# Two graph-attention layers, 64 graphs on one core: scores of the last attention in four banks, placed weight preparation, a new order of the work

## The chip, the cores and the metric

One core of a Trainium2 chip runs the whole program. The metric is device time in microseconds. TensorE (PE) multiplies matrices into PSUM, which has eight banks of 512 fp32 columns on 128 partitions; VectorE (DVE) and ScalarE (ACT) read PSUM and SBUF; GpSimd (POOL) works in SBUF alone; SyncE (SP) issues most DMAs. Each engine follows its own instruction list and waits on semaphores.

## What is computed

64 graphs of 128 nodes with 256 features each, and a 128 x 128 adjacency matrix for each graph. For each graph:

```python
h = relu(layernorm(x))
# first layer (GAT): 4 heads of 128; scores = leaky_relu(asrc + adst), masked, softmax; elu
# second layer (GAT): 1 head of 256, the same with other weights
x = x + gat2(elu(gat1(h)))
h = relu(layernorm(x))
# multi-head attention: 8 heads of 32, masked by adj
q, k, v = h @ Wq, h @ Wk, h @ Wv
out = relu(softmax(mask(q k^T / sqrt(32))) @ v)
x = x + out @ Wo
```

## The kernel before

The work on one graph is cut into some 75 small functions, each on one engine: `project1` (h times W1), `transpose_ab`, `scores1_mask`, `scores1`, `transpose1`, `aggregate1`, `project2`, `scores2`, `transpose2`, `aggregate2`, `qk`, `project_v`, `scores3_mask`, `scores3_first`, `scores3_last`, `mha_av`, `project_out` on TensorE. Between them ACT and DVE take results out of PSUM and do softmax, and GpSimd does a power for the layer norm (`rsqrt1`, `rsqrt2`), masks, a normalisation (`normalise`), a diagonal matrix (`diagonal2`) and the rounding of the exponentials (`e3_first_halves`, `e3_last_halves`).

Each engine runs one loop of steps. A hand-written list gives the order of its functions in a step and, as a number, the phase: in step t a function with phase p works on graph t - p. So each step works on up to a dozen graphs, and the order in a list is the order in which that engine issues. The steps of two engines are not tied to each other but by semaphores: `done` waits for the same graph's input, `free` for a buffer of a ring of two, and `after(pe, sem, g, lag)` for what has to have been read out of a PSUM bank before the function writes to it.

Matrix products in fp16 use numbers split into a high and a low half (`SPLIT`, three products for each). The halves of h, h2, the attention output and the exponentials e3 are turned by DMA transposes on SP's queue (`norm1_transpose`, `norm2_transpose`, `att_transpose`, `e3_transpose_first` and `_last`).

The last attention runs as follows. `qk` makes q and k transposed in one bank; `qk_copy` (ACT, L487) writes their high half and `qk_low` (DVE, L724) the low half; `scores3_mask` writes the mask into two banks, `scores3_first` and `scores3_last` add the scores of four heads each. A head has 32 channels, so its matmul uses a strip of 32 of the array's rows, and the two banks take turns:

```python
for col in columns:
    for n, (i, j) in enumerate(SPLIT):
        for b in range(2):
            h = head_at(4 * b + col)
            r = slice(DK * (h % 4), DK * (h % 4 + 1))
            pe.matmul(S[:, b, col * N:(col + 1) * N], qkT[r, ...], qkT[r, ...])
```

`mha_max` (DVE, L756 and L761) takes the maxima of all eight heads, `mha_exp_first` and `mha_exp_last` (ACT, L497) the exponentials, the e3 halves (POOL, L372 and L374) split them, and `mha_av` multiplies with v. `relu2` (ACT, L482) takes z from `norm2_apply` (DVE, L631), which follows `residual1` (L738), `norm2_moments` and `variance2`.

The weights are prepared in the first steps, by functions that stand between two steps (`before={...}`): `prepare_w1` and `prepare_w2` find the largest weight (`power_of_two`, with two small matmuls of `spread_largest`), scale and split.

## Time and profile before

| | |
|---|---|
| median of 3 runs | 776.16 us (776.13 to 776.79) |
| profiled execution | 774.69 us, its span 772.6 us |
| TensorE busy | 716.3 us, 93% of the span, 8398 matmuls |
| weight loads busy | 593.4 us, 77% |
| DVE busy | 681.4 us, 88% |
| ACT busy | 591.6 us, 77% |
| GpSimd busy | 515.8 us, 67% |
| mean DMA rate | 110 GB/s |

The span is the stretch that the profiler records, from the first instruction to the last. Matmuls overlap, so the duration of one is longer than its share of the time; the spacing of starts is what counts. ACT and DVE instructions overlap a little too: the next starts some 0.1 us before the one before ends.

### The profile page before, as it was taken

The numbers are of one execution on the slowest core, as the hardware profiler recorded it, in microseconds if no ns is written. First come the engines' busy times: TensorE is split into PE (matmuls) and PEld (weight loads), VectorE is DVE, ScalarE is ACT, GpSimd is POOL, SyncE is SP. The second block draws the span as 40 slices with busy tenths as digits, with TensorE's granted clock in tenths as the row PEclk, the third lists the DMA queues.
The fourth block names the chain that finished last, engine by engine and source line by source line (L and its number), as shares of the span: only waits on it lengthen the run. The fifth ranks groups of instructions, "written<-read, shape, count | busy, mean of one in ns | idle before, by whom it ended". The sixth has DMA issues, their size and how long they took to land.

```text
span 772.6 us, 26496 instructions
## 1 busy us (share of the span) xinstructions
PE 716.3 (93%) x8398; PEld 593.4 (77%) x8398; DVE 681.4 (88%) x2017; ACT 591.6 (77%) x1865; POOL 515.8 (67%) x733
## 2 busy tenths in 40 slices
PE   0389999999999999999999999999999999999973
PEld 0157788888888888888888888888888888788852
DVE  4758899999999999999999999999999989999873
ACT  0167888888888778888888788788888888788752
POOL 5456777676767676667667766676677767766551
PEclk9999999999999999999999999999999999999996
DMA  6111555666578566557766656766655666655464
GB/s 197 33 37 43 106 112 112 121 110 118 118 117 115 116 112 113 119 114 115 122 110 118 112 124 115 115 110 120 114 119 116 113 119 106 112 118 105 89 110 89
DMA packets 270423, 84.70 MB, mean 110 GB/s; under 512 B 242896, under 2 KB 269904, under 8 KB 270288
## 3 DMA queue, kind: packets, MB, share of 16 engines
q1 hardware_dynamic: 270288, 83.02, 57.8%
q8 instruction: 70, 1.15, 0.7%
q14 instruction: 65, 0.53, 0.3%
HBM read 15.86 MB, written 8.39 MB: 31 GB/s over the span
## 4 chain that ended last, share of the span: by engine, by line
PE 75%; DVE 9%; DMA 5%; issue 4%; SPq 3%; ACT 1%; POOL 1%; DVEq 0%; ACTq 0%; POOLq 0%
PE bank L815 28%; PE bank L840 11%; PE bank L986 7%; PE bank L947 6%; DMA hT<-h_split 4%; PE bank L966 3%; PE bank L929 3%; PE bank L936 3%; PE bank L866 3%; PE bank L891 2%; PE bank L889 2%; PE bank L881 2%; SPq L276 1%; DVE top L756 1%; PE bank L874 1%
## 5 line engine op out<-in xcount | busy, mean ns | idle before, releaser
L497 ACT ACTIVATE e<-bank,nmx,q_power 128x128 f32<-128x128 f32 x512 | 194.7, 481 | 5.1 <-DVE nmx L761 5.1
L372 POOL CAST e_split<-e 128x512 f16<-128x512 f32 x128 | 82.4, 643 | 118.6 <-ACT e L497 118.6
L374 POOL TENSOR_TENSOR e_split<-e,e_split 128x512 f16<-128x512 f32 x128 | 151.7, 1185 | 10.3
L840 PE MATMUL bank<-w,h1T 128*128 128x258 f32 x512 | 122.8, 382 | 0.7 <-DVE shift L599 0.7
L386 POOL TENSOR_TENSOR rstd<-var,minus_half 128x1 f32<-128x1 f32 x128 | 71.7, 560 | 66.6 <-DVE var L625 66.6
L815 PE MATMUL bank<-w_split,hT 128*128 128x260 f16 x768 | 98.2, 278 | 12.3 <-DMA hT<-h_split 11.9
L840 PEld LDWEIGHTS bank<-w,h1T 128*128 128x128 f32 x512 | 96.6, 190 | 16.6 <-DVE h1T L655 1.6
L448 ACT ACTIVATE eT<-lr,nmx 128x128 f32<-128x128 f32 x256 | 102.7, 458 | 0.8 <-DVE nmx L713 0.8
L815 PE MATMUL bank<-h2T,proj_split 128*128 128x128 f16 x1536 | 97.4, 220 | 1.6 <-DMA h2T<-h_split 1.6
L815 PEld LDWEIGHTS bank<-h2T,proj_split 128*128 128x128 f16 x1536 | 92.0, 99 | 3.7 <-DMA h2T<-h_split 2.4
L815 PEld LDWEIGHTS bank<-w_split,hT 128*128 128x128 f16 x768 | 71.1, 98 | 24.5 <-issue 7.0
L364 POOL TENSOR_TENSOR eTn<-eT,rs 128x512 f32<-128x512 f32 x64 | 67.0, 1046 | 17.9 <-DVE rs L752 17.9
L756 DVE TENSOR_REDUCE top<-bank 128x8 f32<-128x1024 f32 x64 | 77.3, 1208 | 0.3 <-PE bank L947 0.3
L424 ACT ACTIVATE h_split<-z 128x256 f16<-128x256 f32 x64 | 26.6, 416 | 65.9 <-DVE z L631 65.9
L947 PEld LDWEIGHTS bank<-qkT 32*128 32x128 f16 x1536 | 43.0, 93 | 37.7 <-issue 36.0
L986 PE MATMUL bank<-en,xl 128*128 128x128 f32 x512 | 68.3, 276 | 0.2
L448 ACT ACTIVATION_READ_ACCUMULATOR eT<-lr,nmx 128x1 f32 x256 | 65.7, 257 | 0.0
L947 PE MATMUL bank<-qkT 32*128 32x128 f16 x1536 | 64.8, 216 | 0.3 <-DVE qkT L724 0.2
L986 PEld LDWEIGHTS bank<-en,xl 128*128 128x128 f32 x512 | 62.2, 192 | 2.0 <-ACT en L455 1.3
L604 DVE SCALAR_TENSOR_TENSOR h_split<-z,h_split 128x256 f16<-128x256 f32 x128 | 61.5, 481 | 0.6 <-ACT h_split L424 0.5
L815 PE MATMUL bank<-proj_split,attT 128*128 128x256 f16 x384 | 54.3, 279 | 6.1 <-DMA attT<-att_split 6.1
L440 ACT ACTIVATE lr<-bank,ab 128x128 f32<-128x128 f32 x64 | 23.5, 368 | 43.6 <-PE bank L867 43.6
(116 smaller groups left out, 1921.7 us busy)
## 6 DMA issues: line engine op xcount, KB each, us to landing
x_in<-in_x_dram SPq DMA_DIRECT2D x64, 128.0 KB, 2.3
out_dram<-x_out SPq DMA_DIRECT2D x64, 128.0 KB, 2.0
adj_in<-in_adj_dram SPq DMA_DIRECT2D x64, 64.0 KB, 2.5
e3T<-e_split SPq DMA_TRANSPOSE x128, 3.1
hT<-h_split SPq DMA_TRANSPOSE x64, 2.4
h2T<-h_split SPq DMA_TRANSPOSE x64, 2.5
attT<-att_split SPq DMA_TRANSPOSE x64, 2.8
w<-in_L_gnn_W_dram SPq DMA_DIRECT2D x2, 256.0 KB, 3.1
```

What stands on the lines that cost most here:

```text
L364: pool.tensor_tensor(eTn[:, g.two, :].rearrange("p (h n) -> p h n", h=H), eT[:, g.two, :].rearrange("p (h n) -> p h n", h=H), rs[:, g.two, ...
L372: pool.tensor_copy(e3_split[:, g.two, half, 0], e).then_inc(s[high_set], 1)
L374: pool.tensor_tensor(e3_split[:, g.two, half, 1], e, e3_split[:, g.two, half, 0], ALU.subtract).then_inc(s[low_set], 1)
L386: pool.tensor_tensor(rstd[:, g.two, which:which + 1], var[:, g.two, which:which + 1], minus_half[:, :], ALU.pow).then_inc(s[rstd_set], 1)
L448: ins = act.activation(eT[:, g.two, h * N:(h + 1) * N], lr[:, g.two, h * N:(h + 1) * N], ACT.Exp, bias=nmx[:, g.two, h:h + 1], accum_out=s ...
L497: ins = act.activation(e3[:, g.two, h, :], S[:, h // 4, (h % 4) * N:(h % 4 + 1) * N], ACT.Exp, bias=nmx3[:, g.two, h:h + 1], scale=q_power ...
L604: dve.scalar_tensor_tensor(out=out_, in0=in_, scalar=0.0, in1=high_, op0=ALU.max, op1=ALU.subtract).then_inc(s[sem_], 1)
L756: dve.tensor_reduce(top3[:, g.two, :], S.rearrange("p b (h n) -> p (b h) n", h=4), AX.X, ALU.max, negate=True).then_inc(s["top3_set"], 1)
L815: ins = pe.matmul(out_, left, right, start=n == 0, stop=n == len(pairs) - 1)
L840: ins = pe.matmul(X2[:, 0:D + 2], h1T[:, g.two, k * F:(k + 1) * F], w2[:, k, :], start=k == 0, stop=k == H - 1)
L947: ins = pe.matmul(S[:, b, col * N:(col + 1) * N], qkT[r, g.two, i, h // 4, :], qkT[r, g.two, j, 2 + h // 4, :], start=False, stop=n == 2 a ...
L986: ins = pe.matmul(O1[:, h * N:(h + 1) * N], xl[:, g.two, h * F:(h + 1) * F], en[:, g.two, h * N:(h + 1) * N], start=True, stop=True)
```

## The change

**Scores in four banks.** S becomes the first half of banks 0 to 3. Bank b takes the two heads whose channels lie in row strip b, so four consecutive matmuls use four strips and four banks. Half a score stage is one half of the heads (0 to 3, 4 to 7). The other tiles are given other banks: some that had a bank for themselves now share one.

**Order.** All five lists are new, and phases with them. TensorE's first function is now `project1`, with phase 0. `scores3_first` and `scores3_last` stand side by side, between `transpose1` and `aggregate1`.

**Weight preparation** is cut into functions with a place of their own in the lists, each run once, at graph 0. W1 is loaded first; the attention vectors and b1 of the first layer go by ACT's queue and have their own semaphores.

```diff
-        XL = bank[:, 0:2, :]
-        ABT = bank[:, 2, 0:N // 2].bitcast(F16)
-        Z = bank[:, 3]
+        XL = bank[:, 4:6, :]
+        ABT = bank[:, 1, 0:N // 2].bitcast(F16)
+        Z = bank[:, 7]
         ET = bank[:, 6]
-        O1 = bank[:, 1]
+        O1 = bank[:, 6]
         X2 = bank[:, 6]
-        Z2 = bank[:, 7]
-        ET2 = bank[:, 6]
-        O2 = bank[:, 2]
-        QK = bank[:, 7]
-        V = bank[:, 3]
-        S = bank[:, 4:6, :]
-        AV = bank[:, 2]
-        WO = bank[:, 0]
...
+        Z2 = bank[:, 3]
+        ET2 = bank[:, 4]
+        O2 = bank[:, 4]
+        QK = bank[:, 6]
+        V = bank[:, 4]
+        S = bank[:, 0:4, 0:2 * N]
+        AV = bank[:, 7]
+        WO = bank[:, 5]
...
             steps(lambda graphs: run([
-                (e3_transpose_last, 9), (att_transpose, 10), (store, 11), (norm1_transpose, 3), (e3_transpose_first, 8),
-                (load_adj, 1), (load_x, 0), (norm2_transpose, 6),
+                (norm2_transpose, 8), (e3_transpose_last, 9), (load_adj, 4), (norm1_transpose, 4), (e3_transpose_first, 9),
+                (att_transpose, 10), (load_x, 0), (store, 11),
             ], graphs))
...
-                (e3_last_halves, 9), (masks, 3), (e3_first_halves, 8), (rsqrt1, 2), (rsqrt2, 6), (diagonal2, 5),
-                (normalise, 4),
...
+                (masks, 6), (split_low2, 10), (rsqrt1, 4), (rsqrt2, 9), (split_low3, 11), (split_low0, 9),
+                (e3_last_halves, 10), (split_low1, 9), (products_w2, 5), (picks, 2), (products_w1, 2), (diagonal2, 8),
+                (e3_first_halves, 10), (normalise, 7),
...
-                (v_copy, 9), (relu1, 3), (gat2_leaky, 6), (att_copy, 10), (abT_copy, 4), (gat1_copy, 5), (gat2_exp, 6),
-                (gat1_leaky, 4), (mha_exp_first, 8), (elu_exp, 5), (gat2_copy, 6), (mha_exp_last, 8), (qk_copy, 7),
-                (gat1_exp, 4), (relu2, 6),
...
+                (gat1_copy, 7), (gat1_leaky, 6), (elu_exp, 7), (relu2, 8), (split_high0, 7), (mha_exp_last, 9),
+                (split_high2, 8), (mha_exp_first, 9), (gat1_exp, 6), (abT_copy, 5), (gat2_leaky, 7), (relu1, 3), (v_copy, 9),
+                (gat2_exp, 7), (qk_copy, 8), (gat2_copy, 7), (split_high1, 7), (att_copy, 10), (split_high3, 8),
...
-                (xl2_evac, 6), (relu2_low, 7), (ab_high, 4), (v_low, 9), (ab_low, 4), (xl_evac, 4), (gat2_scores, 6),
-                (mha_max, 8), (att_low, 10), (relu1_low, 3), (residual2, 11), (norm1_moments, 2), (gat1_scores, 4), (elu, 5),
-                (gat2_recip, 6), (variance1, 2), (residual1, 6), (norm2_moments, 6), (variance2, 6), (qk_low, 7),
-                (ab2_evac, 5), (norm2_apply, 6), (gat1_recip, 4), (att_norm, 9), (norm1_apply, 2),
...
+                (v_low, 10), (proj_largest, 7), (relu1_low, 4), (gat2_recip, 8), (qk_low, 9), (w1_sums, 2), (att_low, 11),
+                (residual1, 8), (proj_row, 7), (w1_largest, 0), (w1_row, 3), (w2_shift, 7), (w1_scale, 4), (norm2_moments, 8),
+                (variance2, 8), (mha_max, 9), (norm2_apply, 8), (proj_scale, 7), (elu, 7), (relu2_low, 8), (b1_prep, 5),
+                (gat1_scores, 6), (ab_high, 5), (ab_low, 5), (w2_sums, 5), (xl_evac, 5), (norm1_apply, 3), (w1_products, 0),
+                (ab2_evac, 7), (att_norm, 10), (residual2, 11), (xl2_evac, 7), (variance1, 2), (norm1_moments, 1),
+                (gat1_recip, 6), (gat2_scores, 7),
...
             def scores3_mask(g):
                 done(pe, s["masks_set"], g)
-                after(pe, s["e3_last"], g, -1)
-                wide = mask_mha[:, g.eight, :].unsqueeze(1).to_broadcast((128, 4, N))
-                for b in range(2):
-                    ins = pe.matmul(S[:, b, :].rearrange("p (h n) -> p h n", h=4), ident16[:, :], wide, start=True, stop=False)
+                after(pe, s["e3_first"], g, -1)
...
+                wide = mask_mha[:, g.eight, :].unsqueeze(1).to_broadcast((128, 2, N))
+                for b in range(4):
+                    ins = pe.matmul(S[:, b, :].rearrange("p (h n) -> p h n", h=2), ident16[:, :], wide, start=True, stop=False)
                 ins.then_inc(s["s_mask"], 1)
...
+                for n, (i, j) in enumerate(SPLIT):
+                    for b in range(4):
+                        r = slice(DK * b, DK * (b + 1))
+                        ins = pe.matmul(S[:, b, chunk * N:(chunk + 1) * N], qkT[r, g.two, i, chunk, :], qkT[r, g.two, j, 2 + chunk, :],
+                                        start=False, stop=n == 2 and chunk == 1)
...
             steps(lambda graphs: run([
-                (scores3_mask, 8), (scores3_first, 8), (scores2, 6), (scores3_last, 8), (transpose_ab, 4), (transpose1, 5),
-                (scores1_mask, 4), (scores1, 4), (project_out, 11), (aggregate1, 5), (transpose2, 6), (project_v, 8), (qk, 7),
-                (aggregate2, 6), (project2, 5), (mha_av, 9), (project1, 3),
-            ], graphs), before={0: lambda: spread_largest(0, 0, 2, 2), 4: lambda: spread_largest(1, 2, 6, 3)})
+                (turn_w1, 0), (spread_w1, 0), (project1, 0), (project2, 2), (w2_ones, 1), (project_out, 6), (transpose_ab, 0),
+                (project_v, 4), (scores2, 2), (qk, 3), (scores3_mask, 3), (transpose2, 2), (scores1_mask, 0), (scores1, 0),
+                (aggregate2, 2), (transpose1, 1), (turn_proj, 1), (scores3_first, 3), (scores3_last, 3), (aggregate1, 1),
+                (mha_av, 4), (spread_proj, 1),
+            ], graphs))
```

## Rows read from the trace of the kernel before

**Rows 1.** The chain that ended last, at two places: start us, us, what.

```profile
77.11 1.00 PE bank L815 x9
...
714.70 1.34 PE bank L815 x12
```

**Rows 2.** Timeline of PE: start us, us, engine, line, operation, out<-in, shape, count.

```profile
26.00 2.76 PE L815 MATMUL bank<-w_split,hT 128*128 128x260 f16 x12 [6.99 <-DMA hT<-h_split]
...
207.95 1.49 PE L815 MATMUL bank<-w_split,hT 128*128 128x260 f16 x12
209.27 0.59 PE L936 MATMUL bank<-mask_mha,ident 128*128 128x512 bf16 x2
209.80 0.51 PE L947 MATMUL bank<-qkT 32*128 32x128 f16 x12
210.24 0.49 PE L866 MATMUL bank<-diag,ones 128*128 128x128 f32 x2
...
211.22 0.60 PE L966 MATMUL bank<-ident,eTn 128*128 128x128 f32 x4
...
218.81 1.49 PE L815 MATMUL bank<-w_split,hT 128*128 128x260 f16 x12
```

**Rows 3.** Timeline of ACT in the same step.

```profile
208.26 0.42 ACT L482 ACTIVATE h_split<-z 128x256 f16<-128x256 f32 x1
208.58 0.37 ACT L492 ACTIVATE vv<-bank 128x256 f16<-128x256 f32 x1
...
211.86 0.60 ACT L455 ACTIVATE en<-bank 128x512 f32<-128x512 f32 x1 [0.16 <-PE bank L966]
212.36 0.39 ACT L471 ACTIVATE eT<-lr,nmx 128x128 f32<-128x128 f32 x1
...
212.74 0.68 ACT L433 ACTIVATE lr<-bank,power 128x512 f32<-128x512 f32 x1
...
215.41 1.55 ACT L497 ACTIVATE e<-bank,nmx,q_power 128x128 f32<-128x128 f32 x4
216.78 0.67 ACT L487 ACTIVATE qkT<-bank 128x512 f16<-128x512 f32 x1
217.26 0.48 ACT L448 ACTIVATE eT<-lr,nmx 128x128 f32<-128x128 f32 x1
...
218.71 0.26 ACT L448 ACTIVATION_READ_ACCUMULATOR eT<-lr,nmx 128x1 f32 x1
```

**Rows 4.** Timeline of DVE in the same step.

```profile
211.69 1.21 DVE L756 TENSOR_REDUCE top<-bank 128x8 f32<-128x1024 f32 x1
212.93 0.32 DVE L761 TENSOR_SCALAR nmx<-top,q_power 128x8 f32<-128x8 f32 x1
213.16 0.41 DVE L766 TENSOR_TENSOR att_split<-att,att_split 128x256 f16<-128x256 f32 x1
...
216.66 0.48 DVE L738 SCALAR_TENSOR_TENSOR x<-bank,rs,x_in 128x256 f32<-128x256 f32 x1 [0.42 <-PE bank L929]
217.18 0.43 DVE L617 BATCH_NORM_STATS2 stats<-x 128x6 f32<-128x256 f32 x1
...
217.94 0.69 DVE L724 TENSOR_TENSOR qkT<-bank,qkT 128x512 f16<-128x512 f32 x1
```

**Rows 5.** The tile z: durations in ns, min/median/max, first and last start us.

```profile
L631 DVE TENSOR_SCALAR z<-x,mv,rstd x64: 404/646/673, 58.1 to 743.6; 128x256 f32<-128x256 f32 x64
```

**Rows 6.** The page's costliest groups: busy us, mean ns of one, idle before.

```profile
L372 POOL CAST e_split<-e 128x512 f16<-128x512 f32 x128 | 82.4, 643 | 118.6 <-ACT e L497 118.6
L374 POOL TENSOR_TENSOR e_split<-e,e_split 128x512 f16<-128x512 f32 x128 | 151.7, 1185 | 10.3
```

**Rows 7.** The page's DMA issues: count, median us from issue to landing.

```profile
e3T<-e_split SPq DMA_TRANSPOSE x128, 3.1
```

**Rows 8.** Timeline of SP's queue.

```profile
215.50 1.19 SPq L263 DMA_TRANSPOSE hT<-h_split  x1
```

**Rows 9.** The chain that ended last, in the first 30 us.

```profile
4.19 6.85 DMA b_all<-in_L_gnn_b_dram
```

More of the change, by code:

```diff
@@ L231, in run, with once, first @@
                     function(graphs[phase])
+        def once(function):
+            def first(g):
+                if g.n == 0:
+                    function(g)
+            return first
         block = ctx.enter_context(nc.Block())
@@ L333, in picks, with products_w1 @@
                                        pattern=[[-H, 2], [-1, 2], [0, 128]], channel_multiplier=1).then_inc(s["pick_set"], 1)
-            def products_w1():
-                pool.wait_ge(s["w1_in"], 16 * 5)
+            @once
+            def products_w1(g):
+                pool.wait_ge(s["w1_in"], 16 * KD)
+                pool.wait_ge(s["att1_in"], 16 * 2)
                 for k in range(KD):
@@ L549, in prepare_w1, with rows_of_largest @@
-            def prepare_w1():
-                dve.wait_ge(s["w1_in"], 16 * 5)
-                dve.wait_ge(s["ident_set"], 5)
-                dve.tensor_reduce(largest[:, 0:1], w1[:, :, :, high], AX.XYZ, ALU.max, apply_absolute_value=True).then_inc(s["largest_set"], 1)
+            def rows_of_largest(n, first, last):
+                rows, column = last - first, list(turned).index(n)
+                dve.wait_ge(turned[n], 1)
+                dve.tensor_reduce(row_largest[0:rows, column:column + 1], PREP[n][0:rows, 0:128], AX.X, ALU.max).then_inc(row_set[n], 1)
+                dve.wait_ge(row_set[n], 1)
+                dve.tensor_scalar(largest_diag[0:rows, first:last], ident[0:rows, 0:rows], row_largest[0:rows, column:column + 1], None,
+                                  ALU.mult).then_inc(diag_set[n], 1)
@@ new lines, in powers_of_two @@
+            def powers_of_two(n, first, last):
+                dve.wait_ge(spread[n], 1)
+                dve.tensor_scalar(power[:, first:last], PREP[n][:, 128:128 + last - first], 2.0 ** -60, None, ALU.max).then_inc(power_set[n], 1)
+                dve.wait_ge(power_set[n], 1)
+                bits = power[:, first:last].bitcast(I32)
+                dve.tensor_scalar(bits, bits, 0x7f800000, None, ALU.bitwise_and).then_inc(power_set[n], 1)
+                dve.wait_ge(power_set[n], 2)
+                dve.tensor_scalar(scale[:, first:last].bitcast(I32), bits, -1.0, float(254 << 23), ALU.mult, ALU.add).then_inc(scale_set[n], 1)
@@ L553, in prepare_w1, with w1_largest, w1_products @@
+            @once
+            def w1_largest(g):
+                dve.wait_ge(s["w1_in"], 16 * KD)
+                dve.tensor_reduce(largest[:, 0:1], w1[:, :, :, high], AX.XYZ, ALU.max, apply_absolute_value=True).then_inc(s["largest_w1"], 1)
+            @once
+            def w1_products(g):
+                dve.wait_ge(s["w1_in"], 16 * KD)
+                dve.wait_ge(s["att1_in"], 16 * 2)
                 for k in range(KD):
@@ L785, in _, with turn_w1 @@
         @block.tensor
         def _(pe):
[L787 removed]
+            @once
+            def turn_w1(g):
                 pe.wait_ge(s["ident_set"], 5)
[L790 to L796 removed]
@@ new lines, in turn_proj, with spread_proj @@
+            @once
+            def turn_proj(g):
+                pe.wait_ge(s["ident_set"], 5)
+                pe.wait_ge(s["largest_proj"], 1)
+                at_ends(pe, s["e3_first"], g, -2)
+                pe.transpose(PREP["proj"][0:4, 0:128], largest[:, 2:6], ident[:, :]).then_inc(turned["proj"], 1)
+            @once
+            def spread_proj(g):
+                pe.wait_ge(s["ones_set"], 4)
+                pe.wait_ge(diag_set["proj"], 1)
+                pe.matmul(PREP["proj"][:, 128:132], ones[0:4, :], largest_diag[0:4, 2:6], start=True, stop=True).then_inc(spread["proj"], 1)
```

253 lines of the change are left out of this document (157 added, 96 removed).

## Prediction

> **What bounds the kernel now.** I read the page first (TensorE is busy for 93% of the span), then the chain that ended last, then one graph's step on each engine in order of time. The long middle is a pipeline with one graph per step: the first projection of graph 5 starts at 77.1 us and that of graph 63, the last, at 714.7 [rows 1], so 58 steps take 637.6 us, 10.99 each. A step in which TensorE's rows show no idle time takes 218.81 - 207.95 = 10.86 us [rows 2]. The 0.13 on top comes in single late steps. So the step is set by TensorE's issue order. Around it lie 77.1 us of fill and 772.6 - 714.7 = 57.9 us of drain. The reader should see three parts: 77.1 + 58 x 10.99 + 57.9 = 772.6, the span. The profiled execution took 774.69, so 2.1 lie outside the span, and the median of the runs (776.16) is 1.5 above that.
>
> **How full is a step?** TensorE has slack nowhere, but another loop is nearly as long. Scores need q and k rounded by ACT and DVE, the maximum needs the scores, the exponentials need the maximum, and ACT rounds the next graph's q and k only after them. Before: the maximum starts at 211.69, that graph's exponentials are followed by qk_copy at 216.78 (5.09 later, 0.67 long), qk_low starts at 217.94, and the next maximum 10.86 - (217.94 - 211.69) = 4.61 after that [rows 3, 4]. 5.09 + 0.67 + 4.61 = 10.37: this loop has only some 0.5 us of slack. That number decides the case.
>
> **Four strips.** Twelve strip matmuls take 210.24 - 209.80 = 0.44 us, with a change of tiling in it. Columns go by at one price: twelve matmuls of 260 columns take 209.27 - 207.95 = 1.32, 0.11 each, so 128 columns are 0.055 and two of 512 are 0.43. The entry gap is then 209.80 - 209.27 - 0.43 = 0.10 [rows 2]. Six pairs at 0.055 are 0.33, and the exit 0.10. So pairs overlap fully today. With four strips and four banks it would be three rounds for a half, six instead of twelve for a graph: 6 x 0.055 = 0.33 us saved. The trace shows no four at once; the lower bound is no gain, the upper 0.33. I take 0.33, since pairs reach the full factor of two. scores2 no longer stands between the halves, so two of the four tiling changes go: 2 x 0.10 = 0.20. The mask goes from two matmuls of 512 columns to four of 256: the same columns, nothing. TensorE's own step: 10.86 - 0.33 - 0.20 = 10.33.
>
> **The wait that takes part of it back.** aggregate1 reads en, which ACT copies after transpose1. Today scores1_mask, scores1 and project_out lie between them. In the new order only the two score halves do. transpose1 starts at 211.22, the copy ends at 211.86 + 0.60 = 212.46 [rows 2, 3], 1.24 after. New: four transposes 0.44 (512 columns of fp32 at twice the price) + change 0.10 + scores 0.33 + change 0.10 = 0.97, so 0.27 of waiting. With no gain from four strips it would be 1.30 and no waiting. So whether four strips overlap moves the step by only 0.06: TensorE's step is between 10.60 and 10.66.
>
> **The other loop in the new order.** I lay out all that stands in it, from the start of the maximum. DVE: maximum 1.24 (212.93 - 211.69), nmx3 0.23 (213.16 - 212.93) [rows 4]; then norm2_apply, which now stands between them and ACT's exponentials, because relu2 is placed ahead of mha_exp_last and needs z: 0.40 to 0.65 (shortest and median) [rows 5]; handover 0.04. ACT: relu2 0.32 (208.58 - 208.26), eight exponentials 2 x 1.37 = 2.74 (216.78 - 215.41), gat1_exp 218.71 - 217.26 + 0.09 = 1.54, abT_copy 0.15 (estimate, a short copy; at most gat2_leaky's), gat2_leaky 0.27 (an estimate: as v_copy), relu1 0.32 (as relu2), v_copy 0.27 (its 0.37 less the overlap of 0.10 that relu2's rows show), gat2_exp 0.38 (212.74 - 212.36), qk_copy 0.67 [rows 3]: together 6.66. gat1_exp and relu2 stood behind qk_copy before; now they stand ahead. DVE again: handover 0.03, qk_low 0.60 (its 0.69 less the 0.09 by which nmx3's successor overlaps it), att_low 0.34 (an estimate: a 256-column operation of 0.41, as its row has it, less 0.07), residual1 0.52 (217.18 - 216.66), moments and variance 217.94 - 217.18 = 0.76 [rows 4]: 2.25 with the handover. The shortest loop is 1.24 + 0.23 + 0.41 + 0.04 + 6.66 + 2.25 = 10.83, with the median z it is 11.07. So qk_low no longer has 4.61 us of DVE work behind it, but 2.2; from the maximum's start to the end of qk_copy it is 1.92 + 6.66 = 8.58, where it was 5.09 + 0.67 = 5.76. This loop, not TensorE, sets the new step. I take 10.95, the middle. TensorE then idles some 0.3 to 0.6 us a step, mostly at scores3_first (qkT) and aggregate1 (en).
>
> By the Trainium skill (SBUF — State Buffer, section "Who interferes with whom") a DVE tensor_scalar in a two-port mode and a GpSimd instruction lock each other out of a shared port pair. The spread of z between 0.40 and 0.65 agrees with that. In the new order GpSimd has rsqrt2 behind it and waits for mha_exp_last when norm2_apply runs, so by that rule z would take 0.41 and the step would be 10.83, 7 us less over 58 steps than my sum.
>
> **Other moved work that I cost at nothing.** hT is now transposed more than a step ahead of project1, which takes away the late steps (the 0.13). The e3 halves take 0.64 + 1.19 each on GpSimd [rows 6] and their transposition lands 3.1 after issue [rows 7]; the last lands near the start of mha_av, see the rivals. ABT, Z2, XL, V, O2 and ET2 now share banks with other tiles, but their evacuations lie a step earlier, in DVE and ACT time that is in the loop already.
>
> **Fill.** Today DVE waits for w1_in until 4.19 + 6.85 = 11.04, the landing of b1's broadcast, which w1_in counts though nothing of W1 needs it [rows 9]; the first projection starts at 26.0 [rows 2], 15 later. New: W1 goes first, the attention vectors and b1 go by ACT's queue, b1 has its own semaphore, the first maximum needs W1 alone, and relu1_low is placed ahead of the splits, so hT's DMA is hidden by them. I take 4 from the earlier start and 3 from the hidden relu1_low and DMA: project1 at 19. The five steps after it take 77.1 - 26.0 = 51.1; there DVE stands in line for GpSimd's prod2 products. Placed in pieces, each needed later, I take 4 off, between 0 and 8. In all 11, so graph 5 at 66. The bounds are 3 (the broadcasts still late, the placed pieces as long) and 15. **Drain.** project1 is now first in its step, not last, but there are three steps fewer behind it: 57.9 as before, plus or minus 3.
>
> **Sum.** 66 + 58 x 10.95 + 57.9 = 759.0; with 2.1 and 1.5 it is 762.6, and I say 762.
>
> **Rivals.** (1) TensorE stays the bound and all of its saving comes through, at 10.65: the loop through ACT is shorter than I sum, since no row shows these neighbours together. 66 + 617.7 + 57.9 + 3.6 = 745. For it: TensorE alone is bound today. Against: the loop today was found from the same rows and fits. (2) The shared port rule holds at each step: 10.83, so 755.6. (3) Slower: mha_av waits. exp_last is done at 1.92 + 0.32 + 1.37 + 0.13 = 3.7 after the maximum's start, GpSimd does the last half until 5.6, diagonal2, then the first until 7.9; SP issues norm1_transpose (1.19) ahead of it [rows 8], so issue at up to 9.0 and landing at 12.1. mha_av's place is near 11.4. What is late there goes through project1, project2, project_out, project_v and qk to qk_copy, that is into the loop; over two steps it adds half of what it is late. At a step of 11.3 the time is 66 + 655.4 + 57.9 + 3.6 = 783. It decides from (776.2 - 3.6 - 123.9)/58 = 11.18 on, so when the landing is later by another 0.5. (4) The middle as I say and the fill shortened by 4 only: 770. (5) The change does not do what it says: four strips go by two at a time. By the terms above the time is the same, because aggregate1 waits for en anyway; only a trace tells it from my forecast.
>
> **How the numbers follow.** Forecast (10.9 to 11.05 a step) 0.40, (1) 0.20, (2) 0.15, (3) 0.15, (4) 0.10; (5) has 0.3, inside the others. The range 743 to 778 takes in (1), (2), (4) and the near half of (3). Below 0.2% (1.6 us) this kernel's runs cannot tell a change. Faster 0.83, same 0.04, slower 0.13.
>
> **What the profile would show.** Right: strip matmuls in 0.35 a graph with nothing between the halves; TensorE idle in the middle with qkT (DVE) and en (ACT) as releasers; step 10.9 to 11.0; first project1 near 19, graph 5 near 66. Wrong: a step under 10.7, or waits of mha_av for the e3T DMA at the head of the list, or graph 5 after 72.

## The result, and the profile after

The changed kernel takes 831.9 us (830.08 to 834.44, 4 runs) beside 776.14 (775.66 to 776.79) for the kernel before on the same chip: 1.072 times as long, 95% interval 1.069 to 1.075. The forecast was 762, range 743 to 778. The sign was wrong. All times are medians of executions in the faster of the chip's two states; one execution of b1_et_bank5 (969 us, granted clock 0.705) fell in the slower state and is left out.

The page of the changed kernel: span, busy time, then the chain by engine and by line.

```profile
span 830.5 us, 27002 instructions
...
PE 718.0 (86%) x8526; PEld 583.0 (70%) x8526; DVE 706.6 (85%) x2017; ACT 598.5 (72%) x1865; POOL 510.9 (62%) x733
...
PE 30%; DMA 19%; DVE 13%; POOL 11%; ACT 10%; issue 9%; SPq 8%; POOLq 0%; ACTq 0%; DVEq 0%
```

TensorE's busy time hardly moved (716.3 before), its share fell from 93% to 86%. VectorE's grew by 25.2 us (681.4 before), and the rounding of the normalised rows alone grew by 25.9 (L693: 87.4 us, where the same instruction, L604 of the kernel before, took 61.5). The rest of the longer span is waiting. The chain names no one engine: DMA, GpSimd and SP's queue hold 38% of it together. That is how a kernel looks whose step is set by loops through several engines.

The first projections, from TensorE's timeline (graph 0, graph 5) and from the chain (graph 63), which answer to [rows 1] and the first row of [rows 2]:

```profile
24.65 2.57 PE L925 MATMUL bank<-w_split,hT 128*128 128x260 f16 x11 [7.64 <-DVE w_split L645]
...
75.23 1.38 PE L925 MATMUL bank<-w_split,hT 128*128 128x260 f16 x11
```

```profile
769.52 1.34 PE bank L925 x12
```

Between graphs 5 and 63 lie 694.3 us, 11.97 a step. The 57.9 us by which the span grew are: fill 75.2 - 77.1 = -1.9, 58 steps x (11.97 - 10.99) = +56.7, drain 61.0 - 57.9 = +3.1. So it is the step. A step is the time from one graph's first projection to the next one's; fill is what lies before graph 5, drain what lies behind graph 63.

The chain that ended last, 25 us from the middle (start us, us, what):

```profile
305.70 1.23 SPq L274
306.99 3.66 DMA adj_in<-in_adj_dram
310.72 0.54 POOL absent L433
...
312.52 1.06 POOL rstd L418 x2
313.60 0.43 DVE z L720
...
314.72 1.15 ACT e L550 x3
...
316.62 1.22 POOL e_split L406
317.85 1.23 SPq L274
```

It closes on itself: e3_transpose_last (L274) at 305.70 and again at 317.85, 12.15 later. In between: SP issues load_adj behind e3_transpose_last, the adjacency lands, GpSimd makes the masks from it, both rsqrt stand behind the masks in GpSimd's list, norm2_apply needs rsqrt2, ACT's exponentials stand behind relu2 which needs z, GpSimd splits the exponentials, and only then can SP issue the next e3_transpose_last. The masks wait for the load in 37 of the 64 graphs, so not every step is 12.15: single steps lie between 10.87 and 13.23, and the mean is 11.97. SP's next row, behind its 1.23 for e3_transpose_last:

```profile
319.13 0.57 SPq L265 DMA_DIRECT2D adj_in<-in_adj_dram  x1
```

The load itself waits for nothing of this; it only stands behind an instruction that does. Phases 4 (load_adj on SP) and 6 (masks on GpSimd) look like two steps of lead. But SP's list has e3_transpose_last with phase 9 and GpSimd's has e3_last_halves with phase 10: SP's step waits for GpSimd's next one. So it is one step, and since the load stands behind that instruction and the masks stand first in the next step, nothing is left of it. Before, both halves had the same phase on both engines (9), and load_adj 1 against masks 3 was two steps.

The longest waits that this and the next loop cause (engine line <- releaser: us in total, times, longest us):

```profile
POOL absent L433 <- DMA adj_in<-in_adj_dram: 41.0, 37, 2.1
PEld bank L967 <- DMA e3T<-e_split: 38.9, 42, 4.0
```

TensorE's timeline around the scores, to be held against the score row of [rows 2]:

```profile
406.79 0.52 PE L1074 MATMUL bank<-qkT 32*128 32x128 f16 x24
407.64 1.13 PE L1115 MATMUL bank<-en,xl 128*128 128x128 f32 x8 [0.33 <-ACT en L508]
```

24 strip matmuls take what 12 took before (0.51): with 0.21 for the last one alone, the starts are (0.52 - 0.21)/23 = 0.013 apart instead of (0.51 - 0.21)/11 = 0.027. Four strips do overlap, and aggregate1 waits 0.33 for en. The ends of matmuls are modelled in a profile, but for the last graph the maximum waits for them, 0.57 after their first start at 810.01:

```profile
810.58 1.22 DVE L843 TENSOR_REDUCE top<-bank 128x8 f32<-128x1024 f32 x1 [0.29 <-PE bank L1074]
```

### The profile page after: what moved, and what is told of

Read it like the earlier page. It is cut to its first block, busy times and chain, and to the rows that moved or that the text cites. A ratio compares the mean times of both kernels' runs of the same rounds, so it can differ in the third digit from the quotient of the medians.

```text
span 830.5 us, 27002 instructions
## 1 busy us (share of the span) xinstructions
PE 718.0 (86%) x8526; PEld 583.0 (70%) x8526; DVE 706.6 (85%) x2017; ACT 598.5 (72%) x1865; POOL 510.9 (62%) x733
## 4 chain that ended last, share of the span: by engine, by line
PE 30%; DMA 19%; DVE 13%; POOL 11%; ACT 10%; issue 9%; SPq 8%; POOLq 0%; ACTq 0%; DVEq 0%
PE bank L925 13%; DMA e3T<-e_split 11%; DMA adj_in<-in_adj_dram 7%; ACT e L550 7%; PE bank L954 5%; POOL e_split L406 4%; SPq L274 4%; DVE top L843 3%; POOL e_split L404 2%; SPq L280 2%; DVE z L720 2%; POOL rstd L418 2%; PE bank L1054 2%; ACT eT L501 1%; PE bank L1065 1%
## 5 line engine op out<-in xcount | busy, mean ns | idle before, releaser
L404 POOL CAST e_split<-e 128x512 f16<-128x512 f32 x128 | 77.9, 609 | 176.2 <-ACT e L550 176.2
L550 ACT ACTIVATE e<-bank,nmx,q_power 128x128 f32<-128x128 f32 x512 | 184.4, 464 | 2.6 <-DVE nmx L848 2.6
L954 PEld LDWEIGHTS bank<-w,h1T 128*128 128x128 f32 x512 | 92.9, 192 | 17.1 <-DVE h1T L744 5.2
L1115 PE MATMUL bank<-en,xl 128*128 128x128 f32 x512 | 72.3, 284 | 23.5 <-ACT en L508 23.5
L508 ACT ACTIVATE en<-bank 128x512 f32<-128x512 f32 x64 | 38.2, 597 | 74.2 <-PE bank L1093 74.1
L693 DVE SCALAR_TENSOR_TENSOR h_split<-z,h_split 128x256 f16<-128x256 f32 x128 | 87.4, 683 | 0.5 <-ACT h_split L535 0.5
L513 ACT ACTIVATE ex<-bank,minus_one 128x512 f32<-128x512 f32 x64 | 44.0, 687 | 49.0 <-PE bank L1115 49.0
L967 PE MATMUL bank<-vv,e3T 128*128 128x33 f16 x512 | 46.1, 179 | 30.8 <-DMA e3T<-e_split 30.3
L967 PEld LDWEIGHTS bank<-vv,e3T 128*128 128x128 f16 x512 | 40.4, 96 | 39.0 <-DMA e3T<-e_split 38.9
L433 POOL TENSOR_SCALAR absent<-adj_in 128x128 f32<-128x128 int32 x64 | 39.3, 614 | 41.5 <-DMA adj_in<-in_adj_dram 41.0
```

What stands on the lines that cost most here:

```text
L404: pool.tensor_copy(e3_split[:, g.two, half, 0], e).then_inc(s[high_set], 1)
L550: ins = act.activation(e3[:, g.two, h, :], S[:, h % 4, (h // 4) * N:(h // 4 + 1) * N], ACT.Exp, bias=nmx3[:, g.two, 2 * (h % 4) + h // 4:2 ...
L693: dve.scalar_tensor_tensor(out=out_, in0=in_, scalar=0.0, in1=high_, op0=ALU.max, op1=ALU.subtract).then_inc(s[sem_], 1)
L954: ins = pe.matmul(X2[:, 0:D + 2], h1T[:, g.two, k * F:(k + 1) * F], w2[:, k, :], start=k == 0, stop=k == H - 1)
L967: pe.matmul(AV[:, o:o + DK + 1], e_high, vv[:, g.two, 0, h, :], start=True, stop=False)
L1115: ins = pe.matmul(O1[:, h * N:(h + 1) * N], xl[:, g.two, h * F:(h + 1) * F], en[:, g.two, h * N:(h + 1) * N], start=True, stop=True)
```

## The experiments

Times are in us, with the ratio to the kernel before on the same chip and its 95% interval. Kernels with the same letter ran on one chip; the kernel before took 776.1 beside the changed kernel, 774.1 beside a, 774.0 beside b, 775.5 beside c, 774.4 beside e and 773.3 beside f. So up to 3 us of a difference between two letters can be the chip's.

| kernel | us | ratio |
|---|---|---|
| after | 831.9 | 1.072 (1.069 to 1.075) |
| a1_adj_step_earlier | 818.6 | 1.057 (1.053 to 1.060) |
| a2_adj_before_e3 | 809.3 | 1.046 (1.043 to 1.049) |
| a3_two_strips | 824.9 | 1.068 (1.063 to 1.072) |
| a4_adj_two_strips | 821.8 | 1.062 (1.057 to 1.067) |
| b1_et_bank5 | 830.4 | 1.074 (1.069 to 1.079) |
| b2_adj_et_bank5 | 808.6 | 1.045 (1.042 to 1.048) |
| b3_adj_et_two_strips | 809.0 | 1.046 (1.043 to 1.049) |
| b4_before_halves_together | 772.3 | 0.998 (0.997 to 0.999) |
| c1_relu1_low_moved | 820.2 | 1.058 (1.056 to 1.061) |
| c2_relu2_behind | 935.6 | 1.207 (1.204 to 1.211) |
| c3_c2_adj_back | 937.4 | 1.208 (1.205 to 1.212) |
| c4_products_w2_later | 807.2 | one run |
| e1_xl2_early | 800.6 | 1.035 (1.031 to 1.039) |
| e2_c1_xl2_early | 802.1 | 1.036 (1.033 to 1.040) |
| e3_xl2_adj_back | 828.4 | 1.071 (1.067 to 1.076) |
| e4_relu1_low_behind_qk | 808.7 | 1.047 (1.041 to 1.052) |
| f1_e3_ahead_of_norm1 | 801.8 | 1.039 (1.033 to 1.045) |
| f2_e3_ahead_xl2_early | 797.7 | 1.033 (1.030 to 1.036) |

### The adjacency's place

a2 puts the load ahead of the transposition it stood behind; a1 leaves it there and issues it a step earlier.

```diff
-                (norm2_transpose, 8), (e3_transpose_last, 9), (load_adj, 4), (norm1_transpose, 4), (e3_transpose_first, 9),
+                (norm2_transpose, 8), (load_adj, 4), (e3_transpose_last, 9), (norm1_transpose, 4), (e3_transpose_first, 9),
```

```diff
-                (norm2_transpose, 8), (e3_transpose_last, 9), (load_adj, 4), (norm1_transpose, 4), (e3_transpose_first, 9),
+                (norm2_transpose, 8), (e3_transpose_last, 9), (load_adj, 3), (norm1_transpose, 4), (e3_transpose_first, 9),
```

> The changed kernel with load_adj kept at phase 4, but placed ahead of e3_transpose_last in SyncE's list instead of behind it. Theory A: the load no longer waits for the rounding of the exponentials, so it is issued about 1.5 us or more earlier and the loop is cut at the same place: as with a step earlier, 775 to 795 us. If it is not the order in the queue but the landing time of the load itself that is long (3.7 us in the middle, beside a median of 2.2), the step falls by less than half of that. Theory B: 825 to 835 us.

> The changed kernel with one number changed: load_adj has phase 3 in place of 4 on SyncE, so each adjacency matrix is loaded one step earlier; the ring of four has room for it. Theory A (a loop through SyncE's queue sets the step: e3_transpose_last, load_adj behind it, landing, masks, rsqrt1 and rsqrt2, norm2_apply, relu2, mha_exp_last, e3_last_halves, e3_transpose_last): that loop is cut, the step falls from 11.97 to the next loop, 11.0 to 11.3, and the time from 832 to 775 to 795 us. Theory B (mha_av waiting for the landing of the first e3 transposition, rival 3 of the prediction, costs the step): nothing of it is touched, 825 to 835 us.

a2 gives back 22.6 us, a1 13.3 (20 and 12 by the ratios). Both miss the 775 to 795 that theory A gave them, and the 825 to 835 of theory B. In both the masks' wait for the adjacency is gone from the head of the list of waits. What a1 has first among waits for a DMA, against 38.9 in the changed kernel:

```profile
PEld bank L967 <- DMA e3T<-e_split: 37.1, 37, 3.8
```

So in a1 mha_av's wait for the transposed exponentials, my rival 3, is left nearly whole. In a2 it falls to 16.8 us (18 times), and a2 is the faster one by 9.3. a1 keeps load_adj's 0.57 in SP's queue ahead of e3_transpose_first, a2 does not; that fits, though no run separates it from the rest.

e3 and c3 put the load back into two later kernels.

> e1 with load_adj behind e3_transpose_last again, as the change has it. The adjacency loop (e3_transpose_last 1.23, adjacency landing 3.67, masks and both rsqrt on GpSimd, z, relu2, the three exps, e_split, e3_transpose_last again) has nothing of xl2_evac in it: 11.9 to 12.1 a step, 826 to 834. If xl2_evac's place was part of what made the adjacency loop long, it is faster than 820.

> The kernel before it in this list with load_adj back behind e3_transpose_last, as in the change. Its loop (e3_transpose_last, load_adj, landing, masks, rsqrt1, rsqrt2, norm2_apply, relu2) still ends in relu2, but mha_exp_last is no longer behind relu2, so the loop is cut on ACT's side: 0 to +8 us over that kernel. If GpSimd's own order carries it on (rsqrt2, then e3_last_halves): +15 to +30 us.

e3 is 27.8 us above e1 and near the changed kernel: with the load at its new place, what else was mended is not seen. c3 is as c2 within their spread (937.4 and 935.6): where another loop is longer (13.7 a step there), the place costs nothing. In these two pairs loops do not add; the longest counts.

### Strips and halves

```diff
-                for n, (i, j) in enumerate(SPLIT):
-                    for b in range(4):
+                for n, (i, j), b in [(n, ij, b) for pair in ((0, 1), (2, 3)) for n, ij in enumerate(SPLIT) for b in pair]:
+                    if True:
```

> The changed kernel with the strip matmuls of scores3 issued for banks 0 and 1 first and then for banks 2 and 3, so that two strips at most run side by side; nothing else. TensorE's score stage grows by 0.33 us a graph. Theory A: TensorE is not in the loop that sets the step, so 0 to +6 us (830 to 838). Rival: what TensorE does longer is paid in full, 64 x 0.33 = +21 us (853).

> load_adj one step earlier and two strips at a time together. Against the kernel with load_adj one step earlier alone: by the prediction's own sum 0.06 us a step at most, since aggregate1 waits for en anyway: 0 to +4 us. Rival: with the adjacency loop cut TensorE is the bound again and all 0.33 us is paid: +21 us.

> As the kernel before it in this list (ET in bank 5, load_adj ahead), and the strip matmuls two at a time. Theory C with the prediction's sum: the score stage is 0.33 us longer, TensorE is not in the loop, 0 to +4 us. Rival (TensorE is now the bound): +15 to +21 us.

None is slower than its partner by more than the spread (824.9 beside 831.9, 821.8 beside 818.6, 809.0 beside 808.6). But the three kernels did not do what their names say. a3's rows, in a step and for the last graph, where the scores start at 802.91:

```profile
414.97 0.53 PE L1074 MATMUL bank<-qkT 32*128 32x128 f16 x24
```

```profile
803.51 1.22 DVE L843 TENSOR_REDUCE top<-bank 128x8 f32<-128x1024 f32 x1 [0.33 <-PE bank L1074]
```

The 24 starts are as dense as with four strips in turn (0.52), and the maximum that waits for them starts 0.60 after the first, where the changed kernel has 0.57. Two strips at a time would have made that 0.90, by my own 0.33. The list gives six matmuls to strips 0 and 1 before six to strips 2 and 3, and yet they overlap nearly as four. How TensorE comes to that, by taking work out of the list's order or by strips that work off queues of their own, is not shown: the rows do not say which strip a start belongs to. So these runs say nothing of what two at a time would cost. That it costs little rests on the wait of 0.33 behind the scores alone.

b4 takes the kernel before and moves scores2 from between the score halves to ahead of them.

```diff
-                (scores3_mask, 8), (scores3_first, 8), (scores2, 6), (scores3_last, 8), (transpose_ab, 4), (transpose1, 5),
+                (scores2, 6), (scores3_mask, 8), (scores3_first, 8), (scores3_last, 8), (transpose_ab, 4), (transpose1, 5),
```

> The kernel before, and only TensorE's order of scores2 changed: it stands ahead of scores3_mask, so that the two halves of the scores follow each other and two of four changes of tiling go. The prediction's sum says 0.20 us a graph, and since TensorE's issue order sets the step of that kernel, 64 x 0.20 = 13 us faster (762 us beside 775); a rival: the loop with 0.5 us of slack and late hT transpositions take it back, 0 to -5 us.

It saves 1.7 us (0.2%), not 13, and lies in the range of the rival (0 to 5 us). The halves are together (timeline):

```profile
407.78 1.08 PE L947 MATMUL bank<-qkT 32*128 32x128 f16 x24
```

Without a gap, 24 starts 0.027 apart and the last one's 0.21 make 0.83; the row has 1.08. The second half waits for the first (the semaphore s_half; the weight loads idle for it 64 times, 15.1 us in all, 0.24 each), since in the two-bank layout its strips write the banks that the first half's other strips write. Before, scores2 filled that time. So most of the 0.20 that I expected of two tiling changes is lost to this wait, and joining the halves is worth 0.2% alone. In the new layout each bank has one strip, and the wait is left out; no run says what joining is worth there.

### Banks

b1 and b2 take ET out of bank 6 (b1 from the changed kernel, b2 from a2).

```diff
-        ET = bank[:, 6]
+        ET = bank[:, 5]
...
-                after(pe, s["qkT_set"], g, -2)
-                at_ends(pe, s["ab2_set"], g, -1)
-                at_ends(pe, s["xl2_set"], g, -1)
+                after(pe, s["x_out_set"], g, -5)
+                after(pe, s["xl_set"], g, 1)
```

> The changed kernel with ET (what transpose1 writes) in bank 5 in place of bank 6, so that transpose1 no longer waits until qk_low has read q and k out of the bank it shares with them, but for the read of WO a step earlier; the load of the adjacency stays where the change put it. Theory C (two loops of nearly the same length: one through SyncE's queue, 12.0 us, one through bank 6: qk_low, transpose1, gat1_copy, aggregate1, elu_exp, relu2, exponentials, gat1_exp, qk_copy, qk_low, 11.5 to 11.8 us): cutting the second alone leaves the first, 820 to 833 us. Theory D (bank 6 alone is the cost): 775 to 795 us.

> ET in bank 5 and load_adj ahead of e3_transpose_last in SyncE's list together. Theory C: both loops are cut and the step falls to the loop that the prediction laid out (maximum, norm2_apply, relu2, exponentials, gat1_exp, qk_copy, qk_low), 10.9 to 11.2 us; with 73 us of fill and 61 of drain 768 to 785 us. If the bank was no cost, it stays at the 809 us of the kernel with load_adj moved alone.

Neither moves anything (830.4 beside 831.9; 808.6 beside 809.3). ET's bank is not what holds the step.

### VectorE's order: relu1_low, relu2, xl2_evac

c1 moves relu1_low from between v_low and qk_low to behind relu2_low (from b2); c2 also moves relu2 behind mha_exp_last on ACT.

```diff
-                (v_low, 10), (proj_largest, 7), (relu1_low, 4), (gat2_recip, 8), (qk_low, 9), (w1_sums, 2), (att_low, 11),
+                (v_low, 10), (proj_largest, 7), (gat2_recip, 8), (qk_low, 9), (w1_sums, 2), (att_low, 11),
...
-                (variance2, 8), (mha_max, 9), (norm2_apply, 8), (proj_scale, 7), (elu, 7), (relu2_low, 8), (b1_prep, 5),
+                (variance2, 8), (mha_max, 9), (norm2_apply, 8), (proj_scale, 7), (elu, 7), (relu2_low, 8), (relu1_low, 4), (b1_prep, 5),
```

```diff
-                (gat1_copy, 7), (gat1_leaky, 6), (elu_exp, 7), (relu2, 8), (split_high0, 7), (mha_exp_last, 9),
+                (gat1_copy, 7), (gat1_leaky, 6), (elu_exp, 7), (split_high0, 7), (mha_exp_last, 9), (relu2, 8),
```

> The kernel with both loops cut (load_adj ahead of e3_transpose_last, ET in bank 5; 809 us, step 11.34 where undisturbed and 11.6 on average), and on DVE relu1_low moved from ahead of qk_low to behind relu2_low. In the place it had, GpSimd rounds or normalises at the same time and relu1_low takes 1.09 us beside 0.42. Theory E (the loop that the prediction laid out sets the step, and relu1_low, which it took as nothing, is its 0.3 us too much, with some tenths of waiting for qk): step 11.0 to 11.1, 808 - 60 x 0.3 to 0.5 = 780 to 792 us. Rival F (the step is set by mha_av waiting for e3T): 800 to 810.

> As the kernel before it in this list, and on ACT relu2 stands behind mha_exp_last instead of ahead of it, so that norm2_apply and its wait no longer stand between the maximum and the exponentials. Theory E: z and handover, 0.5 us, leave the loop: 10.6 to 10.8 a step, 765 to 780 us. Rival: h2T comes 1.4 us later and qk waits for it, or DVE (10.3 us of work a step) is the bound: no gain over the kernel before it.

Both got slower, by 11.6 and 127 us: my theory that only the score loop was left fell. c1's chain shows the loop that I had not seen:

```profile
409.43 0.43 DVE xl L775
...
409.99 1.50 PE bank L925 x24
...
414.49 1.23 DVE top L843
...
421.14 0.42 DVE xl L775
```

xl2_evac (L775) frees the bank that X2 shares with QK; then qk, the mask, scores1 and aggregate2 on TensorE; residual1, the moments, the maximum; and the rest of VectorE's list down to the next xl2_evac: 11.71. What is put into that stretch of VectorE's list makes this loop longer by itself, and relu1_low put in more than its 0.42: norm1_apply, which follows, now runs beside GpSimd's rounding of the exponentials and takes a median of 1.09 (c1's row for it, shortest, median and longest in ns), where b2 has 0.41.

```profile
L720 DVE TENSOR_SCALAR z<-x_in,mv,rstd x64: 396/1091/1179, 15.8 to 736.7; 128x256 f32<-128x256 f32 x64
```

c2 is a case of its own, 115 us above c1. With relu2 behind the exponentials, VectorE waits for it at relu2_low (63.9 us in 63 waits), everything behind that in its list is late, and project_out waits until xl_evac has read the bank that WO shares with XL (140.4 us in 60 waits). Its chain closes through these in 13.41.

e1 (from b2) and e2 (from c1) cut att_norm and residual2 out of it:

```diff
-                (ab2_evac, 7), (att_norm, 10), (residual2, 11), (xl2_evac, 7), (variance1, 2), (norm1_moments, 1),
+                (ab2_evac, 7), (xl2_evac, 7), (att_norm, 10), (residual2, 11), (variance1, 2), (norm1_moments, 1),
```

> The changed kernel with the adjacency load ahead of e3_transpose_last, ET in bank 5, and on VectorE xl2_evac right behind ab2_evac, ahead of att_norm and residual2 (809 us without that last edit). Theory G (a loop through VectorE's order and bank 6: residual1, moments, mha_max, norm2_apply, elu, relu2_low, gat1_scores, xl_evac, norm1_apply, ab2_evac, att_norm, residual2, xl2_evac, then the next graph's qk in X2's bank, the mask and score matmuls, aggregate2, residual1) takes the bank free about 0.9 us sooner; in the kernel without this edit an undisturbed step of 11.34 is set by the score loop with relu1_low's 1.10 in it, and the loop through bank 6 only causes some of the longer steps: mean step 11.60 falls to 11.35 to 11.5, total 797 to 804. Theory S (only the score loop with relu1_low sets the step): no change, 807 to 811.

> As the kernel with relu1_low behind relu2_low (820 us, constant step 11.71, its chain passes xl2_evac, qk, scores, aggregate2, residual1, mha_max, elu, norm1_apply, att_norm, residual2, xl2_evac), with xl2_evac right behind ab2_evac. Theory G: that loop loses att_norm and residual2, 0.88 us by this kernel's chain (xl2_evac at 421.14, ab2_evac's end at 420.26), step 11.71 to between 10.9 and 11.2, total 775 to 795. Rival: the chain shown is only one of several as long (e3T's landing, score loop), gain under 0.3 a step, total 803 to 820.

e1 gains 8.0 us, as the loop through bank 6 said. e2 gains 18.1 on c1: its 802.1 is far above the 775 to 795 of the loop through bank 6 alone and just under the 803 to 820 of the rival, by which several loops are nearly as long. relu1_low's two places then cost the same (800.6 and 802.1), and the chain of both passes e3T's landing.

e4 puts relu1_low behind qk_low (from b2).

```diff
-                (v_low, 10), (proj_largest, 7), (relu1_low, 4), (gat2_recip, 8), (qk_low, 9), (w1_sums, 2), (att_low, 11),
+                (v_low, 10), (proj_largest, 7), (gat2_recip, 8), (qk_low, 9), (relu1_low, 4), (w1_sums, 2), (att_low, 11),
```

> The kernel with the adjacency load ahead and ET in bank 5 (809 us), with relu1_low behind qk_low in place of ahead of it. Theory S (relu1_low's 1.09 us beside GpSimd sits between v_low and qk_low in the score loop): if relu1_low now runs while GpSimd's normalise is over, it takes 0.42 and the step loses up to 0.67, total 775 to 800; if it still takes 1.09 the loop keeps its length, since residual1 stands behind both, total 805 to 812. Theory G alone (bank 6): residual1 is not earlier, no change.

The time stays at 808.7, and so does the mean step (11.60 in both traces), though with a quick relu1_low the forecast was 775 to 800. relu1_low is quick there (second fence, 0.41) where b2 had 1.10 (first fence; the third is b2's GpSimd):

```profile
417.84 1.10 DVE L693 SCALAR_TENSOR_TENSOR h_split<-z,h_split 128x256 f16<-128x256 f32 x1
```

```profile
406.41 0.41 DVE L693 SCALAR_TENSOR_TENSOR h_split<-z,h_split 128x256 f16<-128x256 f32 x1
```

```profile
417.62 1.04 POOL L396 TENSOR_TENSOR eTn<-eT,rs 128x512 f32<-128x512 f32 x1
```

So relu1_low did get shorter, and the mean step did not. e4's chain shows another loop that held it:

```profile
421.11 0.19 PE bank L967
...
426.62 1.51 PE bank L925 x24
...
431.45 1.23 DVE top L843
...
437.08 2.16 SPq L274
...
439.34 1.21 SPq L280
...
440.65 3.26 DMA e3T<-e_split
...
443.96 0.19 PE bank L967
```

mha_av starts at 421.11 and at 443.96: a loop over two steps, 22.85, 11.43 each. In it, norm1_transpose (L280) is issued between the two e3 transpositions.

### e3_transpose_first ahead of norm1_transpose

f1 is e4 with that mended; f2 has e1's edit as well.

```diff
-                (norm2_transpose, 8), (load_adj, 4), (e3_transpose_last, 9), (norm1_transpose, 4), (e3_transpose_first, 9),
+                (norm2_transpose, 8), (load_adj, 4), (e3_transpose_last, 9), (e3_transpose_first, 9), (norm1_transpose, 4),
```

> The kernel with the adjacency load ahead, ET in bank 5 and relu1_low behind qk_low (808.7 us), with e3_transpose_first ahead of norm1_transpose in SyncE's list. Theory R (rival 3 as a loop over two steps: mha_av 421.11, project1, project2, project_out, project_v, qk, qk_copy, residual1, mha_max, exps, e_split, e3_transpose_last, norm1_transpose 1.21 to 2.22, e3_transpose_first with its landing 3.26, mha_av 443.96: 22.85 for two steps, 11.43 each): the loop loses norm1_transpose's place, 1.2 to 2.2, and is 20.7 to 21.6 for two, so the step falls from 11.60 to what the other loops allow, 10.9 to 11.2; total 768 to 786. Rival: the steps of 11.0 to 11.3 beside those of 12.5 are the other loops, and the long ones come from elsewhere (the adjacency or hT, which now lands 1.3 later): 800 to 812.

> f1 with xl2_evac right behind ab2_evac on VectorE. Theory R with the loop through bank 6: with e3T's landing out of the way, what the bank gives shows: 0.1 to 0.3 a step beside f1, 755 to 775. Theory that only TensorE's own order is left after f1: as f1 within 3 us.

f1 gains 6.9 us, f2 another 4.1. Both miss 786 and 775. f1's 801.8 lies in the range of its rival (800 to 812), and e4 and f1 ran on different chips: by the ratios the gain is 5.8, and their intervals overlap (1.041 to 1.052 and 1.033 to 1.045). The mean step agrees with a gain, 11.60 in e4's trace and 11.49 in f1's, and mha_av's waits for e3T fall from 34.1 us to 18.3. But the loop was not cut. In f1's chain the transposition behind the other lands in 4.39 where e4 had 3.26, and there mha_av's starts are still 22.87 apart:

```profile
382.26 0.19 PE bank L967
...
400.70 4.39 DMA e3T<-e_split
...
405.13 0.19 PE bank L967
```

f2's chain from 400 to 440 is the score loop and nothing else, three steps in a row:

```profile
412.99 1.23 DVE top L843
...
414.38 0.42 DVE z L720
...
420.95 0.60 ACT qkT L540
...
422.19 0.42 DVE h_split L693
...
422.96 0.48 DVE x L825
...
424.21 1.23 DVE top L843
```

424.21 - 412.99 = 11.22. It is the loop that the prediction summed, with one instruction that the sum did not have: relu1_low (L693), which e4's edit had put behind qk_low.

### The fill

c4 (from b2) gives GpSimd's products_w2 phase 6 in place of 5.

> ET in bank 5, load_adj ahead, and GpSimd's four products for W2 one step later, so that they no longer run beside w1_scale on DVE. A look at the fill: in the changed kernel the three small steps and the split of W1 took 0.96, 1.10 and 2.69 us beside 0.17, 0.41 and 0.90 before. Theory: they go back to the short durations and the first project1 starts 3 us sooner (21.5 beside 24.6). Rival: their length comes from something else, such as the operands' layout, and stays.

The changed kernel's VectorE in the fill, and GpSimd beside it:

```profile
8.52 1.22 DVE L610 TENSOR_REDUCE largest<-w 128x1 f32<-128x1024 f32 x1 [8.52 <-DMA w<-in_L_gnn_W_dram]
...
17.79 0.96 DVE L603 TENSOR_SCALAR power<-power 128x2 int32<-128x2 int32 x1
...
19.92 2.69 DVE L641 TENSOR_SCALAR w_split<-w,scale 128x1024 f16<-128x1024 f32 x2
```

```profile
17.29 5.29 POOL L362 TENSOR_TENSOR prod<-w,att 128x512 f32<-128x512 f32 x4
```

and c4, with the products out of the way:

```profile
17.72 0.17 DVE L603 TENSOR_SCALAR power<-power 128x2 int32<-128x2 int32 x1
...
18.13 0.99 DVE L641 TENSOR_SCALAR w_split<-w,scale 128x1024 f16<-128x1024 f32 x2
```

With L605, which stands between them (1.10 and 0.17), 0.96 + 1.10 + 2.69 became 0.17 + 0.17 + 0.99: 3.4 us, and the first projection starts at 21.15, not 24.65. But graph 5 starts at 73.3, as in b2 (73.1). What the first graph gains, the next ones wait for; which of them was not followed further.

## Why the prediction was wrong

- **The step that failed: the moved load was never costed.** "Of what is moved" I costed hT, the e3 halves and the banks, and said nothing of load_adj, although the diff shows it behind e3_transpose_last and its lead cut from two phases at one base to two at another. Its loop of 12.15 is above all my terms. Shown by a2 (-22.6 us) and e3 (+27.8). It is not the whole of the 55.8 us: with the load ahead (a2) the kernel is still 35 us slower than the kernel before on its chip, by the loops below.
- **Rival 3 was the right mechanism and came second.** It had 0.15. I put the landing at 12.1 after the maximum's start; in e4's chain it is 443.91 - 431.45 = 12.46, so it is 0.36 later than I said, near the 0.5 from which I said it decides. In e4 it gives 11.43 a step, where I had 11.3. f1 changed the order of the transpositions for 6.9 us without cutting it, so its full price was not measured.
- **The score loop: mechanism right, one term missing.** I summed 10.83 to 11.07 and took 10.95. b2, whose lists of VectorE and ACT are those of the change, shows 421.17 - 409.83 = 11.34 where nothing disturbs a step. The missing term is relu1_low. The new list puts it between v_low and qk_low, beside ACT's gat2_exp and qk_copy, and my sum went from qk_copy straight to qk_low. b2's rows (relu1_low itself starts at 417.84 and takes 1.10, as above):

```profile
418.02 0.60 ACT L540 ACTIVATE qkT<-bank 128x512 f16<-128x512 f32 x1 [0.18 <-PE bank L925]
```

```profile
418.93 0.66 DVE L811 TENSOR_TENSOR qkT<-bank,qkT 128x512 f16<-128x512 f32 x1
```

  qk_low starts 0.31 after the end of qk_copy (418.62), because relu1_low ends only at 418.94. By my own pieces, with my numbers in brackets: from the maximum's start to qk_copy's end 8.79 (8.58), then 0.31 (0.03), from qk_low's start to the next maximum 2.24 (2.22); together 11.34 (10.83). Of the 0.21 on ACT's part, 0.18 is qk_copy waiting for TensorE. With relu1_low at the 0.42 that it takes alone it would have ended at 418.26, ahead of qk_copy, and cost nothing (an estimate from these rows). So what I missed is its price beside GpSimd's normalise. I had named that effect for z and had not asked it of relu1_low. With 0.28 added my 10.95 would have been 11.23, and I had slower than before from 11.18 on: this term turns the sign at the middle of my range. In f2 relu1_low stands behind qk_low and costs its 0.42 in full; the other pieces there are 10.80, and the loop is 11.22. z took 0.41 to 0.43 in the chains, as rival 2 said.
- **"Share banks with other tiles, already in the loop": wrong for bank 6.** X2 and QK share it, so VectorE's place for xl2_evac goes into qk. It is not first in the changed kernel, but it is worth 8.0 us once the load is mended (e1), and it made c1 slower.
- **Four strips: right.** They overlap fully (0.013 between starts), the wait for en that takes most of it back is 0.33 (0.27). TensorE's own step of 10.60 to 10.66 was never reached and so is neither shown nor refuted; single steps of 10.7 in e1 and f2, between longer ones, are the nearest.
- **Two tiling changes for 0.20: too high in the kernel before** (b4, 0.03 a step), as the wait for s_half had been hidden under scores2. In the new kernel it was not measured.
- **hT earlier, no late steps: wrong.** f2's mean step is 11.39 (graph 5 at 72.9, graph 63 at 733.8) with 11.22 in the undisturbed ones, 0.17 of late steps where there were 0.13.
- **Fill: 1.9 gained, not 11.** project1 came at 24.65, not 19. W1's two loads landed a median 6.4 after issue, beside the broadcasts on ACT's queue; before, 3.1. The first maximum starts at 8.52, 2.5 before the 11.04 of [rows 9], where I took 4. So of 24.65 - 19 = 5.7, 1.5 is W1's landing and 3.4 GpSimd; 0.8 is not placed. **Drain** 61.0, just over my 57.9 plus 3.

f2 is 34.2 us below the changed kernel (30 by the ratios). The 24.4 between f2 and the kernel before on its chip are, by f2's trace (span 793.5 beside 772.6): 58 x (11.22 - 10.86) = 20.9 score loop, 58 x (0.17 - 0.13) = 2.3 late steps, -4.2 fill, +1.8 drain, together 20.8 of the 20.9 by which the span is longer. None of the orders tried beats the kernel before. What stays open: what makes f2's late steps (mha_av still waits 20.2 us for e3T there, in 22 graphs, which no further run took away), and whether an order exists in which relu1_low and gat1_exp leave the score loop without lengthening the one through bank 6.

## What to carry to other kernels

When the order of a pipelined kernel is rewritten, list for each engine what stands directly behind every instruction that waits for another engine, loads included, and follow each of them once around until it comes back to itself; the step is the longest such loop, and a sum that follows only the obvious one is a lower bound. Count a load's lead in what its queue waits for, not in phase numbers. With several loops within 10% of each other, mending one shows only the next: the adjacency's 12.15 hid e3T's 11.43, and beside that stood the score loop's 11.34. And do not carry a duration to a new place unasked: what GpSimd does at that moment made relu1_low and norm1_apply 0.41 or 1.09, and moving the one shifted the collision to the other.

## What the runs showed of the hardware

- **Row strips overlap beyond the order of the list.** With four banks, 24 strip matmuls started 0.013 apart even where the list gave six to strips 0 and 1 before six to strips 2 and 3 (0.53 for the 24, beside 0.52 with all four in turn), and a maximum that waits for them started 0.60 after the first, beside 0.57 (a3 and the changed kernel, last graph).
- **VectorE's operations beside GpSimd.** relu1_low, with two inputs in SBUF, took 1.10 when GpSimd's normalise (1.04) had begun 0.22 before it (b2), and 0.41 without (e4). It ended 0.28 after normalise did. norm1_apply, a tensor_scalar of 128x256, took 1.09 when GpSimd's e_split of 1.16 had begun 0.22 before it (c1, 418.88 and 419.10), and 0.41 without (b2). Two 128x2 operations took 0.96 and 1.10 beside GpSimd's products and 0.17 each without. The Trainium skill (SBUF — State Buffer, section "Who interferes with whom") says that a DVE instruction with two SBUF inputs contends with a GpSimd instruction that reads SBUF, and that a two-port operation is blocked for the whole of the other's instruction; the rows agree.
- **A wait can cost clock as well.** In a1, mha_av waited for e3T from about 405 to 408. The granted clock by windows (window: us, PE busy (instructions) and so on, then PEclk, DMA share and GB/s):

```profile
408.00:411.40 3.40, 3.39 (x37) 2.65 (x38) 0.58 (x1) 3.40 (x14) 1.77 (x2) 0.59 0.38 96
```

  and project1 took 2.76 there, where it takes 1.49 at full clock:

```profile
408.63 2.76 PE L925 MATMUL bank<-w_split,hT 128*128 128x260 f16 x12
```

  It ran mostly at the lower level of 1.2 GHz after the wait, 1.3 us on top of it. The mean over the middle was 0.99 in the changed kernel and 1.00 in the kernel before, so this is a small part of its time.
